# Two layer norms centred by a matrix product, half of the q scalings moved to GpSimd, and its tap sums spread over more slots

## The reference

```python
x = x + conv(group_norm(x, 32 groups))   # 1x3, 5-tap row, 7-tap and dilated 5x5 depthwise taps, a 7-shift correlation
t = x as tokens                          # (16, 3136, 64)
t = t + linear_attention(layer_norm(t))  # q, k: elu(.)+1; 16 heads of 64; cos and sin weights; o = qkv / denom
t = t + experts(layer_norm(t))           # softmax over tokens, top 8 tokens of each of 32 experts, two-layer experts
# layer_norm(v): (v - mean(v, -1)) / sqrt(var(v, -1) + 1e-5), over the 64 channels of a token
```

## Time and profile before

| what | value |
|---|---|
| three timed runs | 3574.03, 3574.05, 3577.35 us; median 3574.05 us |
| span of the profiled execution | 3576.8 us |
| PE, DVE, ACT, POOL busy | 89%, 79%, 59%, 43% of the span |
| mean granted TensorE clock | 0.975 |
| DMA engines | 31.8% of 16 engines' span for the kernel's own queue |

### The profile page before, as it was taken

How to read it: one execution, slowest core, us unless ns; L and a number is a source line. 1 busy time by engine, 2 the same in 40 slices (tenths; PEclk the granted TensorE clock), 3 DMA queues, 4 the chain that set the end, 5 groups by cost and what they waited for, 6 DMA issues and landing times.

```text
span 3576.8 us, 44335 instructions
## 1 busy us (share of the span) xinstructions
PE 3179.5 (89%) x16692; PEld 1443.7 (40%) x16692; DVE 2819.0 (79%) x3251; ACT 2126.5 (59%) x2353; POOL 1523.8 (43%) x1078
## 2 busy tenths in 40 slices
PE   3898989988899998989899888999889899899967
PEld 2443344433443335433344334433344333543324
DVE  5987878978787887878779787787878788756864
ACT  1167854777456864678547774468636786444540
POOL 1167612965048631676128651387415762210000
PEclk8999999999999999999999999999999999999987
DMA  1002640055200661026400453006510165203667
GB/s 54 19 1 70 140 102 28 1 116 132 74 19 10 148 136 46 1 61 139 112 28 0 103 130 80 28 1 137 136 48 19 25 144 125 52 1 80 143 159 271
DMA packets 69297, 278.73 MB, mean 78 GB/s; under 512 B 30845, under 2 KB 35485, under 8 KB 64221
## 3 DMA queue, kind: packets, MB, share of 16 engines
q1 hardware_dynamic: 69085, 275.89, 31.8%
HBM read 242.78 MB, written 33.05 MB: 77 GB/s over the span
## 4 chain that ended last, share of the span: by engine, by line
PE 58%; DVE 21%; ACT 7%; issue 7%; DMA 5%; SPq 1%; POOL 1%; DVEq 0%; ACTq 0%; POOLq 0%
PE ps_D L1561 11%; PE ps_C L1495 8%; DVE arena L959 6%; PE ps_E L1540 4%; PE ps_B L1480 4%; PE ps_A L1480 4%; PE ps_D L1495 4%; PE ps_E L1495 4%; DVE region L1130 3%; PE ps_D L1339 3%; DMA RB<-r_keep 3%; PE ps_B L1524 3%; DVE region L1121 3%; PE ps_A L1524 3%; PE ps_A L1358 2%
## 5 line engine op out<-in xcount | busy, mean ns | idle before, releaser
L585 POOL TENSOR_TENSOR arena<-arena,UHL 128x896 f32<-128x896 f32 x525 | 1096.5, 2091 | 416.3 <-ACT UHL L733 415.9
L1561 PE MATMUL ps_D<-region,small 128*128 128x448 f32 x1792 | 773.0, 556 | 62.8 <-DVE OS L1157 36.2
L741 ACT ACTIVATE ps_C<-RB 128x896 f32<-128x896 f32 x448 | 410.8, 917 | 265.0 <-DVE region L1130 198.6
L1130 DVE TENSOR_TENSOR region<-region,ps_C 128x896 f32<-128x896 f32 x448 | 484.5, 1081 | 80.6 <-ACT ps_C L741 78.7
L733 ACT ACTIVATE UHL<-arena,W8C 128x896 f32<-128x896 f32 x525 | 542.2, 1033 | 0.0
L564 POOL TENSOR_SCALAR ST<-ST 128x14 f32<-128x14 f32 x64 | 25.4, 398 | 1082.3 <-DVE ST L1017 1081.0
L1561 PEld LDWEIGHTS ps_D<-region,small 128*128 128x128 f32 x1792 | 320.0, 190 | 365.5 <-issue 241.2
L595 POOL TENSOR_TENSOR UA<-region,CS 128x128 f32<-128x128 f32 (+1 forms) x400 | 230.4, 578 | 363.2 <-PE ps_C L1495 315.1
L1495 PE MATMUL ps_C<-region,UA 128*128 128x512 f32 (+1 forms) x800 | 378.4, 595 | 0.4
L959 DVE SCALAR_TENSOR_TENSOR arena<-arena,W8C 128x448 f32<-128x448 f32 (+1 forms) x235 | 358.4, 1545 | 0.0
L759 ACT ACTIVATE region<-ps_A,NEG 128x1024 f32<-128x1024 f32 (+1 forms) x200 | 222.6, 1113 | 168.1 <-PE ps_A L1480 167.8
(11 more groups left out here) (309 smaller groups left out, 4848.3 us busy)
## 6 DMA issues: line engine op xcount, KB each, us to landing
RB<-r_keep SPq DMA_DIRECT2D x448, 448.0 KB, 5.7
arena<-x SPq DMA_DIRECT2D x8, 1568.0 KB, 6.5
t_keep<-Y SPq DMA_DIRECT2D x7, 1568.0 KB, 5.2
r_keep<-RR SPq DMA_DIRECT2D x448, 7.0 KB, 3.6
w_keep<-region SPq DMA_DIRECT2D x7, 784.0 KB, 5.6
arena<-w_keep SPq DMA_DIRECT2D x4, 784.0 KB, 9.5
arena<-L_ffn_weight SPq DMA_DIRECT2D x1, 2080.0 KB
CST<-cst SPq DMA_DIRECT2D x1, 1568.0 KB, 6.4
```

The costliest lines, as they stand in the source:

```text
L585: pool.tensor_tensor(out=X[:, cut], in0=X[:, cut], in1=PRODUCT[m % 3], op=ALU.add).then_inc(pool_taps.sem, 1)
L741: act.activation(here.area(key)[:, :].rearrange("p (c n) -> p c n", c=2)[:, :, 0:PIX], RB[:, cc].rearrange("p (c n) -> p c n", c=2), ACT.C ...
L1130: dve.tensor_tensor(out=q, in0=q, op=ALU.mult, in1=here.area(key)[:, :].rearrange("p (c n) -> p c n", c=2)[:, :, 0:PIX])\
L1561: ins = pe.matmul(here.area(key)[:, 0:PIX], MW[i][:, c, :], Q[s % 3][:, c, :], start=c == 0, stop=c == NCHUNK - 1)
```

## The change

Three things are done together.

1. A matrix `CEN`, with I - 1/64 in each 64 x 64 diagonal block, takes the place of the identity in `to_tokens`, which is now a matmul. The tokens arrive centred. ACT squares them from PSUM to SQ ahead of its copy; DVE keeps only the sum of squares and the scaling. ACT's square waits until SQ is free (`square_free`). The sums of norm 1's groups 2 and 3 move to k = 1 and 2, their deviations to k = 4 and 6.
2. Chunk pairs 1 and 3 of each step are scaled by POOL, straight from `RB` in SBUF, at slot 9 and 11 after the step's first. ACT's copy and DVE's scaling of these fall away, and PE and SP wait for `pool_scaled` instead.
3. The 45 tap products of the Q stage take three slots of four, 3 to 61, and POOL's sums follow a slot later. DVE's pieces in the drain begin at slot 64.

```diff
-SUM_TILES = [None, None, 1, 5]
-STD_TILES = [None, None, 6, 10]
+SUM_TILES = [None, None, 1, 2]
+STD_TILES = [None, None, 4, 6]
...
-PRODUCT_TILE, PRODUCT_SLOT, POOL_LAG = 20, 3, 4
+PRODUCT_TILE, PRODUCT_SLOT, POOL_LAG, DRAIN_SLOT = 20, 3, 4, 64
+PRODUCT_SLOTS = {PRODUCT_SLOT + n + n // 3: n for n in range(POOL_PIECES - TILE_PRODUCTS)}
...
+POOL_SCALED = {1: 0, 3: 1}
+POOL_SCALE_LAG = {1: 9, 3: 11}
...
+def copied_slot(j):
+    return 0 <= j < SLOTS and j % 4 not in POOL_SCALED
...
@@ SP
                         if s >= 1:
-                            sp.wait_ge(*here.filled(("rb", s - 1, 2 * h + 1)))
+                            for cc in (2 * h, 2 * h + 1):
+                                sp.wait_ge(*(scaled_by_pool(pair, s - 1, cc) if cc in POOL_SCALED
+                                             else here.filled(("rb", s - 1, cc))))
@@ POOL
+            def pool_scale(here, s, cc):
+
+                q = Q[s % 3][:, 2 * cc:2 * cc + 2, :]
+                pool.wait_ge(*here.emptied(("qp", s, cc)))
+                pool.wait_ge(*spread_loaded[cc // 2].at(here.pair, s + 1))
+                pool.tensor_tensor(out=q, in0=q, in1=RB[:, cc].rearrange("p (c n) -> p c n", c=2),
+                                   op=ALU.mult).then_inc(pool_scaled.sem, 1)
...
+                    if here.span == "loop" and j + PRODUCT_SLOT - POOL_LAG in PRODUCT_SLOTS:
+                        tap_sum(TILE_PRODUCTS + PRODUCT_SLOTS[j + PRODUCT_SLOT - POOL_LAG])
+                    for cc in POOL_SCALED:
+                        if slot_of_step(j, POOL_SCALE_LAG[cc]):
+                            pool_scale(here, (j - POOL_SCALE_LAG[cc]) // 4, cc)
@@ ACT
-            def tokens(here, which, g):
+            def tokens(here, which, g, square_free):
...
+                if square_free:
+                    act.wait_ge(*square_free)
...
+                for rows, end in parts:
+                    ins = act.activation(SQ[0:rows, 2 * at:2 * end, :],
+                                         here.area(key)[0:rows, at * P:end * P].rearrange("p (g c) -> p g c", c=C),
+                                         ACT.Square)
+                    at = end
+                ins.then_inc(squares.sem, 1)
...
-                        tokens(here, 1, YT_TILES.index(k))
+                        tokens(here, 1, YT_TILES.index(k), ln1_sums.at(pair, YT_TILES.index(k)))
@@ DVE
-                if part == 0:
-                    dve.wait_ge(*here.emptied(({1: "yt", 2: "yt2"}[which], g)))
-                    link(dve.tensor_reduce(out=st[:, 0], in_=u, axis=AX.X, op=ALU.add))
-                    link(dve.tensor_scalar(st[:, 3], st[:, 0], 1.0 / C, None, ALU.mult))
-                elif part == 1:
-                    link(dve.tensor_tensor(out=u, in0=u, in1=st[:, 3].unsqueeze(2).broadcast_to([P, 2 * m, C]),
-                                           op=ALU.subtract))
-                elif part == 2:
-                    link(dve.tensor_tensor(out=SQ[:, 0:2 * m, :], in0=u, in1=u, op=ALU.mult))
...
-                    for part in range(4):
-                        if j - 1 - part in LN2_SLOTS:
-                            norm_part(here, 2, ln2_sums, LN2_SLOTS[j - 1 - part], part)
+                    if j - 2 in LN2_SLOTS:
+                        norm_sums(squares.at(pair, 3 + LN2_SLOTS[j - 2]), ln2_sums, LN2_SLOTS[j - 2])
...
-                            depthwise(here, pair + 1, Q_PIECES[j % 4], DVE_PIECES) if j < SLOTS + POOL_LAG else \
+                            depthwise(here, pair + 1, Q_PIECES[j % 4], DVE_PIECES) if j < DRAIN_SLOT else \
@@ PE
-                    ins = pe.transpose(here.area(key)[0:r, a * P:(a + 1) * P], Y[:, at:at + r], IDN[:, :])
+                    ins = pe.matmul(here.area(key)[0:r, a * P:(a + 1) * P], Y[:, at:at + r], CEN[:, :],
+                                    start=True, stop=True)
...
-                pe.wait_ge(*here.emptied(("rb", s, cc)))
+                pe.wait_ge(*(scaled_by_pool(here.pair, s, cc) if cc in POOL_SCALED
+                             else here.emptied(("rb", s, cc))))
```

More of the change, by code:

```diff
@@ L607, in pair_of_images @@
                 for j in range(ALL_SLOTS):
-                    if here.span == "loop" and POOL_LAG <= j < POOL_LAG + POOL_PIECES - TILE_PRODUCTS:
-                        tap_sum(TILE_PRODUCTS + j - POOL_LAG)
+                    if here.span == "loop" and j + PRODUCT_SLOT - POOL_LAG in PRODUCT_SLOTS:
[3 more added lines that the diff above has]
+                            pool_scale(here, (j - POOL_SCALE_LAG[cc]) // 4, cc)
                     if j - 5 in LN2_SLOTS:
@@ L706, in back @@
                 for g in range(2):
-                    tokens(here, 1, g)
+                    tokens(here, 1, g, ln1_sums.at(pair, 1) if g else ln2_sums.at(here.pair, NG) if routing else None)
                 if routing:
@@ L779, in pair_of_images @@
                                        ACT.Exp, bias=NEG1[:, 0:1]).then_inc(eq_ready.sem, 1)
-                    if here.span == "loop" and PRODUCT_SLOT <= j < PRODUCT_SLOT + POOL_PIECES - TILE_PRODUCTS:
-                        tap_product(here, pair + 1, TILE_PRODUCTS + j - PRODUCT_SLOT)
+                    if here.span == "loop" and j in PRODUCT_SLOTS:
+                        tap_product(here, pair + 1, TILE_PRODUCTS + PRODUCT_SLOTS[j])
                     if j in LN2_SLOTS and j >= SLOTS:
-                        tokens(here, 2, LN2_SLOTS[j])
-                    if 0 <= j - COPY_LAG < SLOTS:
+                        tokens(here, 2, LN2_SLOTS[j], ln2_sums.at(pair, LN2_SLOTS[j]))
+                    if copied_slot(j - COPY_LAG):
                         spread_out(here, *divmod(j - COPY_LAG, 4))
                     if j in LN2_SLOTS and j < SLOTS:
-                        tokens(here, 2, LN2_SLOTS[j])
+                        tokens(here, 2, LN2_SLOTS[j], ln2_sums.at(pair, LN2_SLOTS[j]) if LN2_SLOTS[j]
+                               else ln1_sums.at(pair, NG))
                     if here.span == "loop" and j in FRONT_SLOTS:
@@ L871, in _ @@
                                    in0=turns[:, :, 0], in1=turns[:, :, 1], op=ALU.add))
+            for half in HALVES:
+                link(dve.tensor_scalar(CEN[half, half], IDN[half, half], -1.0 / C, None, ALU.add))
             link(dve.tensor_tensor(out=BOTH[:, :], in0=IDN[:, 0:C], in1=IDN[:, C:P], op=ALU.add))
@@ L1000, in conv_residual, with norm_sums, norm_scale @@
                 ins.then_inc(*here.empty(key))
-            def norm_part(here, which, sums, g, part):
+            def norm_sums(squared, sums, g):
+                m = GROUPS[g][1]
+                dve.wait_ge(*squared)
+                dve.tensor_reduce(out=ST[:, g % 2, 1, 0:2 * m], in_=SQ[:, 0:2 * m, :], axis=AX.X, op=ALU.add)\
+                    .then_inc(sums.sem, 1)
+            def norm_scale(here, which, std, pair, g):
                 t, m = GROUPS[g]
@@ L1078, in back, with squared @@
                 conv_residual(here, pair, 1)
-                norm_sums(here, 1, ln1_sums, 0)
-                for part in range(4):
-                    norm_part(here, 1, ln1_sums, 1, part)
-                    if part == 1:
-                        norm1_scale(pair, 0)
+                def squared(g):
+                    return squares.first(g + 1) if before is None else squares.at(before, 3 + NG + g)
+                norm_sums(squared(0), ln1_sums, 0)
+                norm1_scale(here, pair, 0)
+                norm_sums(squared(1), ln1_sums, 1)
                 low_part(pair, 0)
                 conv_residual(here, pair, 2)
-                norm1_scale(pair, 1)
+                norm1_scale(here, pair, 1)
                 conv_residual(here, pair, 3)
@@ L1703, in _ @@
                         .then_inc(*end.fill(key))
-VSETUP = 50
-VLOOP = 44
+VSETUP = 44
+VLOOP = 12
 LOW = -3.0e38
```

39 lines of the change are left out of this document (19 added, 20 removed).

## The result

The kernel after the change takes 3528.80 us (median; 3527.94 to 3537.89), the kernel before, on the same chip, 3574.04 us (3571.93 to 3577.35). The ratio is 0.9883, 95% interval 0.9867 to 0.9899: 45 us faster by the medians, 42 by the ratio. The forecast was 3562 us, so the direction holds and the size is short by 33 us.

A forecast was written before the change was run, and what follows sets the result against it. PE was taken to bound the K stage and plain Q steps. Seven loop pairs at -2.0 us, the last pair -4 and pair 0's K start +6 gave -12 us together: 3562 us, range 3510 to 3612.

The forecast's parts named there:

- the last pair: Final pair, without taps: parts removed as well and its end follows the norm, so -4 us.
- PE's pace in plain steps: Q stage: PE fills a plain step, so reciprocals stay 11.6 us apart after the change.
- The product at 0.22 us a tile: Matmul replacing the transpose: 0.22 us a tile against 0.11, so 0.75 us more a group, 5.5 a pair.
- Tail and K start: Tail and start of the K stage: first k_project 2.4 us later, ACT's square waits, +3.5; together +5.9 us a pair.
- The drain's total: End of the Q stage: -3.6 us a pair from DVE's work removed, +0.4 for group 3's product.
- Rival D: ACT's square switches its function table, two switches a group at 1.28 us: 3700 us, chance 0.03.
- the step that has PE's wait for the token copy grow by 0.95 us: Q stage steps with tokens: ACT's copy ends 0.95 us later behind the square, PE's wait near 2 us.
- Worth nothing by itself: Part 3, taps at three slots of four: only makes room for POOL's scalings, no gain of its own.
- I cost it at nothing: Part 2, POOL's scalings: no gain in plain steps, and no cost, with a cover of 1.1 us a step.
- early pieces of the 1 x 5 kernel: Drain: DVE's early pieces and group 2's norm parts go, -4.3 us a pair before +0.75 for the product.
- Rival B: POOL becomes the Q step's bound if an operation with waits exceeds 2.32 us: 50 us slower, 3613 us, chance 0.20.
- Rival A: No wait at the K stage's start, or more won around the norms (drain gaps fully closed): 3531 us, chance 0.22.

The follow-up runs named there:

- e9: Kernel before with part 3 alone: tap products in three slots of four, DVE's drain pieces from slot 64; 3534.55 us, ratio 0.9896.
- e10: Kernel before with part 2 alone: POOL scales chunk pairs 1 and 3, tap products in every slot; 3576.56 us, ratio 1.0010.
- e11: Kernel before with one number changed: DVE's pieces of the 1 x 5 kernel begin at slot 64 instead of 60; 3552.70 us, ratio 0.9956.
- e1: Kernel after without parts 2 and 3, so the centring product and ACT's squares alone; 3569.48 us, ratio 0.9995 to the kernel before.
- e4: Kernel after without part 3: taps one a slot, POOL still scaling chunk pairs 1 and 3; 3544.10 us, ratio 0.9918 to the kernel before.
- e8: Kernel after with POOL scaling chunk pairs 1, 2 and 3, six POOL operations a step; 3532.69 us, ratio 0.9874 to the kernel before.

## Why the prediction was right in direction and short in size

**The sum.** With the prediction's own bookkeeping (a loop pair ends with the next K start), the loop pairs changed by -40.2 us (forecast -14), the last pair by -13.4 (forecast -4), and pair 0's start by +4.3 (forecast +6): -49.3 us, the difference of the two spans. These come from the stage lengths: 7 x (416.19 - 421.58) = -37.7, corrected by pair 0's and the last pair's own tiles 0 to 3 (-6.1, +3.6); the last pair -9.8 - 3.6; pair 0's first exponential 1.8 us earlier, and 6.1 more behind it. The medians differ by 45: the profiled execution of the kernel before, with the lower clock of the two (0.975 against 0.982), was a slow one.

**Right.** PE's pace in plain steps (11.61 us before and after). The product at 0.22 us a tile. The scaling at 2.09 us. Tail and K start: at full clock +2.7 and +3.6 us a pair, for +2.4 and +3.5 forecast, with the wait in its place: ACT's square 2.34 us behind DVE's reduce, PE idle for 2.27, "some 3 us" foretold. (The table has +5.5 in sum: the clock takes 1.7 off the difference of the tails and adds 0.9 to that of tiles 0 to 3. The forecast had no term for the clock.) The step of 14.47 us falls to 11.60, that of 13.56 to 11.61. The drain's total, -3.4 for -3.2 (the forecast's -3.6 and +0.4). Rival D is out: the trace has the same two table loads as before, with squares, exponentials and copies mixed.

**Wrong in the Q stage, the step that has PE's wait for the token copy grow by 0.95 us.** Forecast -4.7 us a pair, measured -7.7 (slots 0 to 55). The two steps with tokens were to become hardly different (-0.5 + 0.95), and became 0.6 us shorter each; the step with a fold and the scaling of a norm lost 1.3, not 0.7. The slot with tokens in the kernel after, ACT and PE:

```profile
1645.91 0.91 ACT L682 ACTIVATE SQ<-ps_A 128x896 f32<-128x896 f32 x1
1646.71 0.91 ACT L687 ACTIVATE un<-ps_A 128x896 f32<-128x896 f32 x1
```

```profile
1643.25 1.80 PE L1418 MATMUL ps_A<-CEN,Y 128*128 128x128 f32 x14
...
1647.68 0.36 PE L1552 MATMUL ps_A<-plane,WQH 128*128 128x448 f16 x1 [1.12 <-ACT un L687]
```

The square is there, 0.8 us ahead of the copy, but PE's wait is 1.12 us, where the earlier trace rows had 1.28 and "near 2 us" was foretold: PE's own longer turn takes up 0.84 us (1.80 against 0.96). The two steps with tokens make 2.2 us of the miss of 3.0, the step with the fold 0.6. The collision with POOL, which the forecast saw in one row (the square of 2.00 us) and held to under 2 us a group with part 1 in, is no part of it. Without part 1 it counts: with the norm's work on DVE unchanged, slots 31 to 55 change by -2.4 us a pair in e9 and by +2.5 in e10.

**Wrong: "Worth nothing by itself", said of part 3, and "I cost it at nothing" of part 2.** Part 3 alone gives 37 us. Some 16 are the drain, where the right waits were read but put down to the norm's parts on DVE and the early pieces together; e11 gives the pieces 2.3 us a pair there, while part 1 alone takes only 0.65 off the drain. Another 17 are slots 31 to 55. The "early pieces of the 1 x 5 kernel" stood in part 1's account and belonged to part 3. Part 2 at nothing was right by itself and wrong beside part 1, where it gives 25. Part 2 alone shortens the drain by 3.0 us and gives it back around the norms. So the forecast had the drain's total nearly right from a wrong assignment, and that was seen only because the parts were run apart.

**Wrong in the last pair, "-4".** It lost 13.4 us: 4.5 in its Q stage, 5.4 in its drain, 3.5 behind it (where the clock is 0.74 before and 0.81 after, so that no part is shown for it). PE's long wait in the drain, in the kernel before, with ACT's copy of RB that it hangs on, and the same 16 products in the kernel after:

```profile
3442.12 9.22 PE L1561 MATMUL ps_D<-region,small 128*128 128x448 f32 x16 [4.98 <-DVE OS L1157]
```

```profile
3438.16 0.92 ACT L741 ACTIVATE ps_C<-RB 128x896 f32<-128x896 f32 x1 [3.08 <-DMA RB<-r_keep]
```

```profile
3399.28 6.28 PE L1590 MATMUL ps_D<-region,small 128*128 128x448 f32 x16 [1.28 <-DVE OS L1185]
```

The wait is 3.7 us shorter, and the products behind it 2.9: in the kernel before the granted clock falls to half at 3441.25, within the wait, and stays there for 6.8 us; in the kernel after it stays full. So it is in every profile: in the six without part 1 PE waits 3.5 to 5.0 us there and the clock falls to half toward the end of the wait, for 3.4 or 6.8 us, in the eight with part 1 it waits 1.3 to 2.6 and the clock stays full. The forecast looked at loop pairs alone for RB, and at no clock. Parts 1 and 2 both shorten this drain (from 33 us to 29.8 in e1, 29.5 in e10, 27.4 in e4), both at least in part by way of the clock.

**Rival B, the threshold.** "It decides where an operation with its waits takes over 11.61 / 5 = 2.32 us" compared POOL with a plain step. e8 runs at 12.6 us a step without loss, and e4 with 0.6 us a pair more in slots 31 to 55 than the kernel after: what POOL is held against is the mean step, near 13 us. **Rival A**'s number, 3531 us, came out, but by neither of its two conditions: the wait at the K start is there in full, and the drain gave hardly more than the forecast. Its heading, "more won around the norms", holds for 3 us a pair; the rest is the last pair. That its number fits is luck.

## What to carry to other kernels

Where an engine empties PSUM and also makes a second result of it, the copy that others wait for goes first; here the order of two instructions was worth 42 to 50 us. A two-input operation of VectorE, and here even one of 14 elements, can't be costed by its own length where GpSimd runs in one row beside it: either it leaves VectorE, or GpSimd gets gaps. An engine that runs beside the bound is held against the mean step, not against the shortest; and a change of three parts is priced with each part both alone and beside the others, for the same edit (part 2) was worth nothing alone and 25 us beside part 1. And two profiles are compared stretch by stretch at the same granted clock: 1.6 us a pair of e11's tail would have been put down to the edit, and at equal clock it is nothing.

## What the runs showed of the hardware

A tiny operation with a single SBUF input (128 x 14, 0.17 us) was held for up to 5.84 us in e10: in each of the seven cases over 3 us it ended within 0.04 us of the end of the last of three GpSimd operations that followed each other without a pause. The reduce just ahead of it (L1034 at 1659.78, also from SBUF) ran beside the same GpSimd work in its usual 1.08 us: it is not the input's place alone that decides.

TensorE's granted clock fell to half toward the end of PE's long wait in the last drain (3.5 to 5.0 us, six profiles of six) and not at the short ones (1.3 to 2.6 us, eight of eight). Behind the wait of 2.3 us at the K start it fell in five of eight pairs of the kernel after. 16 products took 9.22 us in a stretch with 6.8 us at half clock, 6.28 at full.

The small store to `r_keep` (four DMAs of 7 KB) has no fixed price: in pair 3 of the two kernels it lands 1.4 to 5.9 us after its issue. The DMA view of the kernel after, of a step in its first half (1612 to 1617) and of the step behind the tokens (1652 to 1656): the queue's packets, MB and share of 16 engines, and the store with its us to landing:

```profile
q1 hardware_dynamic: 181, 1.07, 101.1%
...
r_keep<-RR SPq DMA_DIRECT2D x4, 7.0 KB, 5.8
```

```profile
q1 hardware_dynamic: 100, 0.02, 2.9%
...
r_keep<-RR SPq DMA_DIRECT2D x4, 7.0 KB, 1.4
```

Where the DMA engines are full with the reloads of the step before, the store takes four times as long, and SP issues the next reload that much later. The median of the whole run fell, from 3.6 us to 2.9 (part 6 of the two pages), but in the third to fifth steps of pair 3 it rose from 3.7 to 4.1 us to 4.8 to 5.9 us. There ACT and POOL wait for RB, POOL's scaling at 1614.49 for 2.45 us. The step with a fold around it (1611.54 to 1625.45) is 1.1 us longer than before (13.91 against 12.81 us). That the one is the cause of the other was not tried by itself.
